# ACT copies a full bank, POOL adds twice: where the output additions of a fused retention and FP4 block are made

## The chip, the cores and the metric

One core of one Trainium2 chip. The metric is the device time of one execution in microseconds. The engines are called PE (TensorE), DVE (VectorE), ACT (ScalarE), POOL (GpSimd) and SP (SyncE, here only a DMA queue).

## The reference

Only what is computed matters here; the full reference also draws the inputs. The input is 8 x 1024 rows of 256 values.

```
x = L0_attn_X
xn = _layernorm(x, axis=-1)
x = x + _L0_attn_ref(xn, ...) + _L0_ffn_ref(xn, ...)
# _L0_attn_ref: retention with 8 heads of 32
Q = _xpos(einsum('bse,hed->bhsd', X, W_Q)); K = _xpos(..., downscale=True); V = ...
scores = einsum('bhsd,bhtd->bhst', Q, K) * D
Y = einsum('bhst,bhtv->bhsv', scores, V)
Yn = ((Y - mu) / sqrt(var + EPS)) * gn_weight + gn_bias
gate = X @ W_G; gate = gate * sigmoid(gate)
return gate * Yn @ W_O
# _L0_ffn_ref: every operand of a product is rounded to FP4 in blocks of 16
h = silu(fp4_linear(x, w_gate)) * fp4_linear(x, w_up)      # 704 wide
return fp4_linear(h, w_down)
```

## The kernel before

The kernel is written engine by engine: each engine has a program of its own, and semaphores tie them together. The order in which an engine works is the order of its code; nothing is scheduled by a planner.

The rows are cut into 64 tiles of 128 rows. Each engine runs `step(i)` for i from -4 to 63, and then `drain()`. A step is a software pipeline over several tiles: step i normalises and rounds tile i+1 or i+2, makes the large products of tile i, the retention and the quantisation of `h` for tile i-1, the down and output projections of tile i-2, and the final additions of tile i-3. Steps 0 to 2 also carry a part of the work on the weights, which the kernel rounds, transposes and splits itself. The weights of gate and up come in parts 0 to 2, those of down in parts 3 and 4. The last tile has no step behind it, so its later stages stand in `drain()`.

Every large product is made three times, with a high and a low part of each operand (`w_gu_hi`, `xqT_lo` and so on), so that fp32 accuracy comes out of the faster format. For the down and output projections the two weight parts lie side by side, `w_dn_both` and `w_out_both`. One product of 512 columns puts the high weights' result into the first half of a PSUM bank (`b_out`) and the low weights' into the second half (`b_out_lo`); both halves together are `b_out2`. The result of a tile is thus `b_out + b_out_lo + x`.

How those three are added is what the change is about. Before, ACT copies the second half into `y_low` (L820), DVE adds the first half and `x_in` into `y_half` (L619 in a step, L765 in the drain), and POOL adds the two into `y_out` (L448). SP then stores `y_out`. The semaphores are `out_ready` (PE has finished the bank), `halved` (ACT has copied), `summed` (the sum with `x_in` is there) and `added` (`y_out` is there). PE may begin the next tile's bank (L1119) when `summed` and `halved` are reached.

Names in the steps that follow: `h_quot` (POOL, L456) divides `h` by its block scale; ACT makes `h_magic` (L852); DVE makes `h_diff` (L691), `h_grid` (L705) and `hq` (L715) from it. `x_inv` (DVE, L695), `x_quot` (POOL, L479), `x_magic` (ACT, L868), `x_diff` (DVE, L711) do the same for the next tile's `x`. `qk` (POOL, L468) is the rotated query and key, which PE transposes at L1149. `y_part` (DVE, L748) and `z` (POOL, L512) end the group norm, `gate_gn` (POOL, L518) prepares it, `probs` (DVE, L759 and L630) masks the scores. `h_inv` (DVE, L632) inverts the block maxima of `h`. All of these stand in SBUF, except that `probs`, `y_half`, `y_part` and the first operand of a low part are read from PSUM.

In the set-up, `divide(n)` multiplies part n of the gate and up weights by its inverse scales, `round_off(n)` puts it onto the grid, and `centre_qkvg` takes the mean out of the projection weights, four column groups on ACT and four on POOL.

Of the kernel before, what the change touches and what calls it, by code (L numbers as in the profile page):

```python
# [16 lines left out]
P = 128  # L17
# [13 lines left out]
SLOTS = 8  # L31
# [37 lines left out]
def block_kernel(nc, x, xT, w_qkvg_d, w_o, gn_d, w_gu_d, w_down_d, cos_d, sin_d, causal_d, ident_d, by_head_d, out):  # L69
# [3 lines left out]
    with ExitStack() as ctx:  # L73
# [93 lines left out]
        y_half = sb("y_half", [P, 2, D])  # L167
        y_low = sb("y_low", [P, 2, D])
        y_out = sb("y_out", [P, 2, D])

# [267 lines left out]
        def _(pool):  # L438
# [4 lines left out]
            def residual(t):  # L443
# [4 lines left out]
                pool.tensor_tensor(y_out[:, t % 2, :], y_half[:, t % 2, :], y_low[:, t % 2, :], ALU.add).then_inc(added, 1)  # L448

            def step(i):  # L450
                if exists(i - 1):
# [22 lines left out]
                if exists(i - 3):  # L474
                    residual(i - 3)
                if exists(i + 1):
# [43 lines left out]
            def drain():  # L520
# [25 lines left out]
            def centre_qkvg():  # L546

                pool.wait_ge(qkvg_mean, 2)
                for j in range(4, 8):
                    pool.tensor_scalar(w_qkvg[:, j, :], w_qkvg[:, j, :], w_mean[:, j:j + 1], None,  # L550
                                       ALU.add).then_inc(qkvg_centred[1], 1)

# [23 lines left out]
        def _(dve):  # L576
# [36 lines left out]

            def first_half(t):
                dve.wait_ge(out_ready, t + 1)
                dve.wait_ge(halved, t + 1)
                if t >= 2:
                    dve.wait_ge(added, t - 1)
                dve.tensor_tensor(y_half[:, t % 2, :], b_out, x_in[:, t % SLOTS, :], ALU.add).then_inc(summed, 1)  # L619

            def step(i):
# [48 lines left out]
                if exists(i + 2):  # L670
                    t = i + 2
                    if t == 0:
                        dve.wait_ge(cleared, 2)
                    dve.wait_ge(x_stats, t + 1)
                    dve.bn_aggr(moments[:, 0:2], stats[:]).then_inc(x_moments, 1)  # L675
                    if i == -2:
                        largest(0)
                        invert(0)
                        divide(0)
                        largest(1)  # L680
                        round_off(0)
                        invert(1)
                        divide(1)
                if exists(i - 2):
# [76 lines left out]
            def residual(t):  # L761
                dve.wait_ge(out_ready, t + 1)
                dve.wait_ge(halved, t + 1)
                dve.wait_ge(added, t - 1)
                dve.tensor_tensor(y_half[:, t % 2, :], b_out, x_in[:, t % SLOTS, :], ALU.add).then_inc(summed, 1)  # L765
# [17 lines left out]
            def drain():  # L783
# [20 lines left out]
                z_low_part(t)  # L804
                residual(t)

# [7 lines left out]
        @block.scalar  # L814
        def _(act):
            def second_half(t):
                act.wait_ge(out_ready, t + 1)
# [4 lines left out]
            def step(i):  # L822
                if exists(i):
# [4 lines left out]
                    if exists(i - 3):  # L828
                        second_half(i - 3)
                    act.wait_ge(x_turned, t + 1)  # L830
                    act.activation(xqT_hi[:], tiles(b_xT[:, 0:D]), ACT.Copy).then_inc(xT_high, 1)
                    if i == 0:
                        low_part(2, 3)
                        high_part(4, 5)
                        qkvg_high_part(2)
                        magnitude(3)
                        qkvg_low_part(2)
                        out_high_parts()
# [16 lines left out]
                if exists(i + 1):  # L855
                    t = i + 1
                    if i == -1:
                        magnitude(0)
                        total_qkvg(0)
                        high_part(0, 1)  # L860
                        centre_qkvg()
                        magnitude(1)
                    if i == 0:
# [3 lines left out]
                    act.wait_ge(x_divided, t + 1)  # L867
                    act.activation(x_magic[:], x_quot[:], ACT.Abs, scale=GROW).then_inc(x_abs, 1)  # L868
                if exists(i):
                    t = i  # L870
# [58 lines left out]
            def drain():  # L929
# [16 lines left out]
                z_high_part(t)  # L946
                second_half(t)

# [35 lines left out]

            def centre_qkvg():

                act.wait_ge(qkvg_mean, 1)
                for j in range(4):
                    act.activation(w_qkvg[:, j, :], w_qkvg[:, j, :], ACT.Identity, bias=w_mean[:, j:j + 1],
                                   scale=1.0).then_inc(qkvg_centred[0], 1)  # L990

# [30 lines left out]
            for i in range(FIRST, 0):  # L1022
                step(i)
            high_part(2, 3)
            for i in range(TILES):
# [4 lines left out]
        def _(pe):  # L1030
# [5 lines left out]
            def step(i):  # L1036
# [16 lines left out]
                if exists(i):  # L1053
# [6 lines left out]
                    ins.then_inc(x_turned, 1)  # L1060
                    if i == 0:
                        turn_rest(2, 3)
                        turn(4, 5)
                        turn_qkvg(2)
                        turn_qkvg_rest(2)
# [42 lines left out]
                if exists(i - 2):  # L1108
# [117 lines left out]
            def turn_h(t):  # L1226
# [5 lines left out]
                ins.then_inc(h1_turned, 1)  # L1232

            def down_first(t):
                pe.wait_ge(hT_high0, t + 1)
                pe.wait_ge(summed, t)
                pe.wait_ge(halved, t)
                for k in range(3):
                    ins = pe.matmul(b_out2, hT_hi[:, k], w_dn_both[:, k], start=k == 0, stop=False)
                ins.then_inc(down_h0, 1)  # L1240

            def down_rest(t):
                pe.wait_ge(hT_high1, t + 1)
                for k in range(3, 5):
                    ins = pe.matmul(b_out2, hT_hi[:, k], w_dn_both[:, k], start=False, stop=False)
# [4 lines left out]
                pe.matmul(b_out2, hT_hi[:, 5], w_dn_both[:, 5], start=False, stop=False).then_inc(down_l1, 1)  # L1250
                pe.wait_ge(hT_low0, t + 1)
# [4 lines left out]
            def project_out(t):  # L1256
                pe.wait_ge(z_high, t + 1)
                for k in range(KD):
                    ins = pe.matmul(b_out2, zT_hi[:, k], w_out_both[:, k], start=False, stop=False)
                ins.then_inc(out_high, 1)  # L1260
# [174 lines left out]
```

## Time and profile before

| what | value |
|---|---|
| time, median of 3 executions | 883.75 us (883.57 to 884.05) |
| the profiled execution's own time | 883.53 us |
| its span | 881.7 us |
| PE busy | 856.0 us (97%) |
| DVE busy | 856.2 us (97%) |
| ACT busy | 462.3 us (52%) |
| POOL busy | 726.8 us (82%) |
| granted PE clock | full speed in all slices |
| HBM traffic | 37 GB/s over the span |

The span is the time from the first to the last event of the profiled execution; the time contains a little around it. Busy is the sum of an engine's operations, whoever waits for them. Two engines show 97% at once, so busy time alone does not say which of them sets the pace; the chain of work and the waits do.

### The profile page before, as it was taken

To read this page: it belongs to the slowest core of one execution; us is meant where nothing else is said; L and a number is where in the kernel's file an instruction comes from. 1 tells how busy PE (TensorE), PEld (TensorE's weight loads), DVE (VectorE), ACT (ScalarE), POOL (GpSimd) and SP (SyncE) were. 2 spreads that over 40 slices of the span, in tenths; PEclk is the share of its full clock that TensorE was granted. 3 is DMA by queue.
4 is the path that set the end of the run, shared out by engine and by line. 5 is a ranking of instruction groups with operands and counts; after the bars stand their busy time and mean duration, and the time that the engine had idled before them with its cause. 6 is when DMAs were issued, how large, how long until landed. Compare 5 with 4: busy or idle time off the path is not lost.

```text
span 881.7 us, 20677 instructions
## 1 busy us (share of the span) xinstructions
PE 856.0 (97%) x7858; PEld 708.7 (80%) x7858; DVE 856.2 (97%) x1883; ACT 462.3 (52%) x1210; POOL 726.8 (82%) x858
## 2 busy tenths in 40 slices
PE   3889999999999999999999999999999999999997
PEld 2668888888888888888888888888888888888885
DVE  7999999999999999999999999999999999999996
ACT  6655455555554555545545555555455554554553
POOL 5878888888888888888888888888888888888886
PEclk9999999999999999999999999999999999999999
DMA  9200110110111011011011011011001101100000
GB/s 339 82 2 19 38 38 19 38 36 21 36 37 29 28 37 33 23 38 37 19 38 37 20 37 37 23 34 37 29 28 36 34 23 38 37 19 26 13 7 25
DMA packets 30050, 33.63 MB, mean 38 GB/s; under 512 B 3328, under 2 KB 28672, under 8 KB 29696
## 3 DMA queue, kind: packets, MB, share of 16 engines
q1 hardware_dynamic: 29808, 32.26, 11.6%
q8 instruction: 62, 1.02, 0.5%
q14 instruction: 36, 0.29, 0.1%
q10 hardware_dynamic: 144, 0.07, 0.0%
HBM read 23.92 MB, written 8.39 MB: 37 GB/s over the span
## 4 chain that ended last, share of the span: by engine, by line
PE 93%; POOL 2%; DVE 2%; ACT 1%; issue 1%; DMA 0%; POOLq 0%; SPq 0%
PE quad L1034 12%; PE quad L1032 12%; PE quad L1033 12%; PE quad L1119 6%; PE bank L1032 5%; PE quad L1213 5%; PE quad L1095 4%; PE bank L1033 3%; PE quad L1203 3%; PE bank L1034 3%; PE quad L1189 3%; PE bank L1149 3%; PE quad L1198 3%; PE quad L1087 2%; PE quad L1075 2%; PE quad L1079 2%
## 5 line engine op out<-in xcount | busy, mean ns | idle before, releaser
L1032 PE MATMUL quad<-w_gu_hi,xqT_hi 128*128 128x512 f32 (+1 forms) x384 | 149.6, 390 | 0.0
L1034 PE MATMUL quad<-w_gu_hi,xqT_lo 128*128 128x512 f32 (+1 forms) x384 | 143.8, 374 | 0.0
L1033 PE MATMUL quad<-w_gu_lo,xqT_hi 128*128 128x512 f32 (+1 forms) x384 | 142.5, 371 | 0.0
L491 POOL TENSOR_TENSOR rstd<-var_eps,power 128x9 f32<-128x9 f32 x66 | 122.7, 1859 | 5.5
L456 POOL TENSOR_TENSOR h_quot<-h,h_inv 128x704 f32<-128x704 f32 x63 | 87.5, 1390 | 5.1
L468 POOL TENSOR_TENSOR qk<-qk_cos,qk_sin 128x512 f32<-128x512 f32 x64 | 83.6, 1307 | 5.9 <-PE bank L1105 0.7
L479 POOL TENSOR_TENSOR x_quot<-xn,x_inv 128x256 f32<-128x256 f32 x64 | 40.5, 633 | 57.8 <-DVE x_inv L695 57.5
L518 POOL TENSOR_TENSOR gate_gn<-gate,gn 128x512 f32<-128x512 f32 x63 | 81.7, 1298 | 0.0
L1034 PEld LDWEIGHTS quad<-w_gu_hi,xqT_lo 128*128 128x128 f32 x384 | 72.1, 188 | 11.4
L1033 PEld LDWEIGHTS quad<-w_gu_lo,xqT_hi 128*128 128x128 f32 x384 | 72.4, 189 | 10.8
L1032 PEld LDWEIGHTS quad<-w_gu_hi,xqT_hi 128*128 128x128 f32 x384 | 72.2, 188 | 11.0
L499 POOL TENSOR_TENSOR xT_lo<-xT_in,xT_hi 128x256 fp32r<-128x256 f32 x64 | 47.7, 745 | 40.4 <-ACT xT_hi L900 40.4
L912 ACT ACTIVATE xn<-x_in,x_shift,rstd 128x256 f32<-128x256 f32 x64 | 38.6, 602 | 77.6 <-POOL x_shift L503 77.6
L705 DVE SCALAR_TENSOR_TENSOR h_grid<-h_magic,h_diff 128x704 f16<-128x704 bf16 x63 | 75.5, 1199 | 0.0
L868 ACT ACTIVATE x_magic<-x_quot 128x256 bf16<-128x256 f32 x64 | 26.7, 417 | 82.8 <-POOL x_quot L479 82.8
L820 ACT ACTIVATE y_low<-quad 128x256 f32<-128x256 f32 x64 | 24.6, 385 | 82.1 <-PE quad L1051 78.5
L691 DVE SCALAR_TENSOR_TENSOR h_diff<-h_magic,h_quot 128x704 f32<-128x704 bf16 x63 | 67.3, 1069 | 0.0
L854 ACT ACTIVATE y_sq<-bank 128x256 f32<-128x256 f32 x63 | 24.2, 384 | 73.7 <-PE bank L1143 73.7
L489 POOL TENSOR_SCALAR var_eps<-moments 128x9 f32<-128x9 f32 x66 | 58.6, 888 | 3.6 <-DVE moments L675 3.2
L1119 PE MATMUL quad<-w_dn_both,hT_hi 128*128 128x512 f32 x186 | 59.7, 429 | 0.0
L1032 PE MATMUL bank<-w_qkvg_hi,xT_hi 128*128 128x512 f32 x128 | 57.1, 446 | 2.0 <-POOL xT_lo L499 1.9
L715 DVE TENSOR_TENSOR hq<-h_grid,h_scale 128x704 f32<-128x704 f16 x63 | 57.0, 904 | 0.0
(224 smaller groups left out, 2738.9 us busy)
## 6 DMA issues: line engine op xcount, KB each, us to landing
x_in<-in_x_dram SPq DMA_DIRECT2D x64, 128.0 KB, 2.2
xT_in<-in_xT_dram SPq DMA_DIRECT2D x64, 128.0 KB, 2.2
out_dram<-y_out SPq DMA_DIRECT2D x64, 128.0 KB, 1.7
sin<-const_sin_dram SPq DMA_DIRECT2D x1, 1792.0 KB, 11.0
raw<-in_w_gu_dram SPq DMA_DIRECT2D x2, 512.0 KB, 6.4
w_qkvg<-in_w_qkvg_dram SPq DMA_DIRECT2D x1, 1024.0 KB, 7.3
cos<-const_cos_dram SPq DMA_DIRECT2D x1, 896.0 KB, 7.1
raw<-in_w_down_dram SPq DMA_DIRECT2D x2, 352.0 KB, 7.8
```

The costliest lines, as they stand in the source:

```text
L456: pool.tensor_tensor(blocks(h_quot[:]), blocks(h[:]), spread(h_inv[:]), ALU.mult).then_inc(h_divided, 1)
L468: pool.tensor_tensor(qk[:], qk_cos[:], qk_sin[:], ALU.add).then_inc(rope_add, 1)
L489: pool.tensor_scalar(var_eps[:], moments[:, 1:], EPS, None, ALU.add).then_inc(var_ready, 1)
L491: pool.tensor_tensor(rstd[:, (t + 3) % RING, 0:1 + H], var_eps[:], power[:], ALU.pow).then_inc(rstd_ready, 1)
L518: pool.tensor_tensor(gate_gn[:, t % 2, :, :], gate[:].unsqueeze(1).broadcast_to([P, 2, D]), gn[:], ALU.mult).then_inc(gate_scaled, 1)
L691: dve.scalar_tensor_tensor(h_diff[:], h_magic[:], LEAST, h_quot[:], ALU.max, ALU.subtract).then_inc(h_diffed, 1)
L705: dve.scalar_tensor_tensor(h_grid[:], h_magic[:], LEAST, h_diff[:], ALU.max, ALU.subtract).then_inc(h_gridded, 1)
L715: dve.tensor_tensor(blocks(hq[:, 0:F]), blocks(h_grid[:]), spread(h_scale[:]), ALU.mult).then_inc(h_quant, 1)
L1032: pe.matmul(out, hi[:, k], w_hi[:, k], start=start, stop=False)
L1033: pe.matmul(out, hi[:, k], w_lo[:, k], start=False, stop=False)
L1034: return pe.matmul(out, lo[:, k], w_hi[:, k], start=False, stop=stop)
L1119: ins = pe.matmul(b_out2, hT_hi[:, k], w_dn_both[:, k], start=k == 0, stop=False)
```

## The change

In steps 3 to 63, ACT copies the whole bank into a new tile `y_both` (L814 of the changed kernel), and POOL makes both additions (L453 and L457). DVE's addition is gone from the step, and PE's wait for it too. The drain keeps the old split for tiles 61 and 62. For the last tile, PE puts the products with the high and the low weights on top of each other into `b_out` (`times_both`, two products of 256 columns for each of 512), and DVE adds `x_in` and writes `y_out` itself.

In the set-up, POOL instead of DVE divides part 1. ACT instead of POOL centres the second half of the projection weights. Three small reorderings on ACT and PE go with it.

The core of the diff (the pieces that only rename a call's place are left out):

```diff
+            def residual_of_both(t):
+                pool.wait_ge(halved, t + 1)
+                pool.tensor_tensor(y_half[:, t % 2, :], y_both[:, t % 2, 0:D], x_in[:, t % SLOTS, :], ALU.add).then_inc(summed, 1)
+                pool.wait_ge(summed, t + 1)
+                if t >= 2:
+                    pool.wait_ge(stored, 16 * (t - 1))
+                pool.tensor_tensor(y_out[:, t % 2, :], y_half[:, t % 2, :], y_both[:, t % 2, D:2 * D], ALU.add).then_inc(added, 1)
+
...
                 if exists(i - 3):
-                    residual(i - 3)
+                    residual_of_both(i - 3)
...
                     if i == -2:
                         size(0)
+                        divide(1)
                     if i == -1:
                         mean_qkvg(1)
-                        centre_qkvg()
...
                 residual(t - 1)
-                residual(t)
...
-                    if exists(i - 3):
-                        first_half(i - 3)
...
                         largest(1)
+                        invert(1)
                         round_off(0)
-                        invert(1)
-                        divide(1)
...
-                residual(t)
+                dve.wait_ge(out_ready, t + 1)
+                dve.wait_ge(added, t)
+                dve.wait_ge(stored, 16 * (t - 1))
+                dve.tensor_tensor(y_out[:, t % 2, :], b_out, x_in[:, t % SLOTS, :], ALU.add).then_inc(added, 1)
...
+            def both_halves(t):
+                act.wait_ge(out_ready, t + 1)
+                if t >= 2:
+                    act.wait_ge(added, t - 1)
+                act.activation(y_both[:, t % 2, :], b_out2, ACT.Copy).then_inc(halved, 1)
...
                     if exists(i - 3):
-                        second_half(i - 3)
+                        both_halves(i - 3)
...
                     if t >= 1:
-                        pe.wait_ge(summed, t)
                         pe.wait_ge(halved, t)
...
+            def times_both(t, part, both, start=False):
+                if exists(t + 1):
+                    return pe.matmul(b_out2, part, both, start=start, stop=False)
+
+                pe.matmul(b_out, part, both[:, 0, :], start=start, stop=False)
+                return pe.matmul(b_out, part, both[:, 1, :], start=False, stop=False)
```

What it does to the order on POOL inside a full step. Before, from `qk` on, between two tiles:

```order
L468 TENSOR_TENSOR qk<-qk_cos,qk_sin 128x512 [waits kv_ready,rope_cos]
L448 TENSOR_TENSOR y_out<-y_half,y_low 128x256 [waits stored,halved,summed]
L479 TENSOR_TENSOR x_quot<-xn,x_inv 128x256 [waits x_inverted]
L489 TENSOR_SCALAR var_eps<-moments 128x9 [waits x_moments,y_var]
L491 TENSOR_TENSOR rstd<-var_eps,power 128x9 [waits var_ready]
```

The same place after:

```order
L477 TENSOR_TENSOR qk<-qk_cos,qk_sin 128x512 [waits kv_ready,rope_cos]
L453 TENSOR_TENSOR y_half<-y_both,x_in 128x256 [waits halved]
L457 TENSOR_TENSOR y_out<-y_half,y_both 128x256 [waits stored,summed]
L488 TENSOR_TENSOR x_quot<-xn,x_inv 128x256 [waits x_inverted]
L498 TENSOR_SCALAR var_eps<-moments 128x9 [waits x_moments,y_var]
```

A second addition now stands between `qk` and `x_quot`, and it waits for the first.

On DVE, the stretch from the rotation's sine part to the low part of the rounded `x`, before:

```order
L632 TENSOR_SCALAR h_inv<-h_rec 128x44 [waits h_recip]
L638 SCALAR_TENSOR_TENSOR qk_sin<-bank,rstd,sin 128x512 [waits qk_ready]
L619 TENSOR_TENSOR y_half<-quad,x_in 128x256 [waits added,halved,out_ready]
L643 TENSOR_TENSOR xqT_lo<-bank,xqT_hi 128x256 [waits xT_high]
L646 SCALAR_TENSOR_TENSOR qk_cos<-bank,rstd,cos 128x512
```

And after:

```order
L626 TENSOR_SCALAR h_inv<-h_rec 128x44 [waits h_recip]
L632 SCALAR_TENSOR_TENSOR qk_sin<-bank,rstd,sin 128x512 [waits qk_ready]
L635 TENSOR_TENSOR xqT_lo<-bank,xqT_hi 128x256 [waits xT_high]
L638 SCALAR_TENSOR_TENSOR qk_cos<-bank,rstd,cos 128x512
L649 BN_STATS stats<-x_in 128x6 [waits loaded0]
```

The addition with `x_in` is gone, and the rest of DVE's step keeps its order.

On DVE in the set-up, where parts 0 and 1 of the gate and up weights (`raw`) are prepared, before:

```order
L580 TENSOR_REDUCE w_max<-raw 128x64 [waits w_landed1]
L598 SCALAR_TENSOR_TENSOR raw<-w_magic,raw 128x768 [waits w_abs]
L601 SCALAR_TENSOR_TENSOR w_magic<-w_magic,raw 128x768 [waits w_rounded0]
L605 TENSOR_TENSOR raw<-w_magic,w_scale 128x768 [waits w_sized,w_rounded0]
L586 RECIPROCAL w_rec<-w_max 128x64 [waits w_scaled1]
L588 TENSOR_SCALAR w_inv<-w_rec 128x64 [waits w_scaled1]
L593 TENSOR_TENSOR raw<-raw,w_inv 128x1024 [waits w_scaled1]
L625 TENSOR_REDUCE x_max<-xn 128x16 [waits x_normed]
```

After:

```order
L581 TENSOR_REDUCE w_max<-raw 128x64 [waits w_landed1]
L587 RECIPROCAL w_rec<-w_max 128x64 [waits w_scaled1]
L589 TENSOR_SCALAR w_inv<-w_rec 128x64 [waits w_scaled1]
L599 SCALAR_TENSOR_TENSOR raw<-w_magic,raw 128x768 [waits w_abs]
L602 SCALAR_TENSOR_TENSOR w_magic<-w_magic,raw 128x768 [waits w_rounded0]
L606 TENSOR_TENSOR raw<-w_magic,w_scale 128x768 [waits w_sized,w_rounded0]
L619 TENSOR_REDUCE x_max<-xn 128x16 [waits x_normed]
```

The inverse scales of part 1 are made before part 0 is rounded, and the division of 1024 columns has left DVE; on POOL it stands behind `size(0)`.

## Rows read from the trace of the kernel before

**Rows 1.** The page's chain that ended last, share of the span by engine.

```profile
PE 93%; POOL 2%; DVE 2%; ACT 1%; issue 1%; DMA 0%; POOLq 0%; SPq 0%
```

**Rows 2.** The chain in order of time: start us, us, what.

```profile
69.46 0.43 PE bank L1032
...
852.99 0.43 PE bank L1032
```

**Rows 3.** Timeline of one full step: start us, us, engine, operation [idle before <-releaser].

```profile
400.15 1.30 POOL L468 TENSOR_TENSOR qk<-qk_cos,qk_sin 128x512 f32<-128x512 f32 x1
...
401.42 0.73 POOL L448 TENSOR_TENSOR y_out<-y_half,y_low 128x256 f32<-128x256 f32 x1
...
401.81 1.09 DVE L691 SCALAR_TENSOR_TENSOR h_diff<-h_magic,h_quot 128x704 f32<-128x704 bf16 x1
...
402.82 0.16 DVE L695 TENSOR_SCALAR x_inv<-x_rec 128x16 f32<-128x16 f32 x1
...
403.06 0.62 POOL L479 TENSOR_TENSOR x_quot<-xn,x_inv 128x256 f32<-128x256 f32 x1 [0.91 <-DVE x_inv L695]
403.23 1.20 DVE L705 SCALAR_TENSOR_TENSOR h_grid<-h_magic,h_diff 128x704 f16<-128x704 bf16 x1
...
403.72 0.42 ACT L868 ACTIVATE x_magic<-x_quot 128x256 bf16<-128x256 f32 x1 [1.26 <-POOL x_quot L479]
...
404.36 0.41 DVE L711 SCALAR_TENSOR_TENSOR x_diff<-x_magic,x_quot 128x256 f32<-128x256 bf16 x1
...
405.27 0.60 ACT L879 ACTIVATE silu<-quad 128x512 f32<-128x512 f32 x1 [0.59 <-PE quad L1034]
...
408.17 0.41 DVE L748 TENSOR_TENSOR y_part<-bank,y_gain 128x256 f32<-128x256 f32 x1
...
408.92 0.73 POOL L512 TENSOR_TENSOR z<-y_part,gate_gn 128x256 f32<-128x256 f32 x1
...
409.07 0.69 DVE L759 TENSOR_TENSOR probs<-quad,causal 128x512 f32<-128x512 f32 x1 [0.16 <-PE quad L1213]
...
409.61 1.31 POOL L518 TENSOR_TENSOR gate_gn<-gate,gn 128x512 f32<-128x512 f32 x1
...
410.60 0.35 DVE L632 TENSOR_SCALAR h_inv<-h_rec 128x44 f32<-128x44 f32 x1
...
411.45 1.39 POOL L456 TENSOR_TENSOR h_quot<-h,h_inv 128x704 f32<-128x704 f32 x1
...
411.54 0.41 DVE L619 TENSOR_TENSOR y_half<-quad,x_in 128x256 f32<-128x256 f32 x1
...
413.28 1.30 POOL L468 TENSOR_TENSOR qk<-qk_cos,qk_sin 128x512 f32<-128x512 f32 x1
...
414.93 1.08 DVE L691 SCALAR_TENSOR_TENSOR h_diff<-h_magic,h_quot 128x704 f32<-128x704 bf16 x1
...
414.98 0.60 PE L1149 MATMUL bank<-ident,qk 128*128 128x128 f32 x4
```

**Rows 4.** Timeline, DVE in step 1 and both engines in the drain.

```profile
49.95 0.86 DVE L691 SCALAR_TENSOR_TENSOR h_diff<-h_magic,h_quot 128x704 f32<-128x704 bf16 x1
...
868.79 1.12 DVE L790 SCALAR_TENSOR_TENSOR h_diff<-h_magic,h_quot 128x704 f32<-128x704 bf16 x1 [0.67 <-ACT h_magic L934]
...
869.13 1.38 POOL L448 TENSOR_TENSOR y_out<-y_half,y_low 128x256 f32<-128x256 f32 x1
```

**Rows 5.** Timeline of the set-up.

```profile
12.14 1.24 DVE L593 TENSOR_TENSOR raw<-raw,w_inv 128x1024 f32<-128x1024 f32 x1
...
13.49 1.69 ACT L989 ACTIVATE w_qkvg<-w_qkvg,w_mean 128x256 f32<-128x256 f32 x4
...
23.11 5.47 POOL L550 TENSOR_SCALAR w_qkvg<-w_qkvg,w_mean 128x256 f32<-128x256 f32 x4
```

**Rows 6.** Timeline of the end.

```profile
877.47 0.40 PE L1263 MATMUL quad<-w_out_both,zT_lo 128*128 128x256 f32 x2
...
878.88 0.72 POOL L448 TENSOR_TENSOR y_out<-y_half,y_low 128x256 f32<-128x256 f32 x1 [3.23 <-DVE y_half L765]
```

More of the change, by code:

```diff
@@ L168, in block_kernel @@
         y_low = sb("y_low", [P, 2, D])
+        y_both = sb("y_both", [P, 2, 2 * D])
         y_out = sb("y_out", [P, 2, D])
@@ L544, in mean_qkvg @@
                 pool.tensor_scalar(w_mean[:, half], w_sum[:, half], -1.0 / D, None, ALU.mult).then_inc(qkvg_mean, 1)
[L546 to L551, printed above, removed]
             def size(n):
@@ L612, in low_difference @@
                     dve.tensor_tensor(lo, shaped(bank[HIGH_BANK[m]]), hi.bitcast(F32), ALU.subtract).then_inc(w_low[m], 1)
[L614 to L619, printed above, removed]
             def step(i):
@@ L763, in residual @@
                 dve.wait_ge(halved, t + 1)
-                dve.wait_ge(added, t - 1)
+                dve.wait_ge(added, TILES - 3 if t == TILES - 3 else t - 1)
                 dve.tensor_tensor(y_half[:, t % 2, :], b_out, x_in[:, t % SLOTS, :], ALU.add).then_inc(summed, 1)
@@ L833, in step @@
                         low_part(2, 3)
+                        qkvg_high_part(2)
                         high_part(4, 5)
-                        qkvg_high_part(2)
                         magnitude(3)
@@ L859, in step @@
                         total_qkvg(0)
+                        magnitude(1)
                         high_part(0, 1)
-                        centre_qkvg()
-                        magnitude(1)
                     if i == 0:
@@ L868, in step @@
                     act.activation(x_magic[:], x_quot[:], ACT.Abs, scale=GROW).then_inc(x_abs, 1)
+                    if i == -1:
+                        centre_qkvg(0)
                 if exists(i):
@@ L946, in drain @@
                 z_high_part(t)
-                second_half(t)
             def magnitude(n):
@@ L983, in total_qkvg, with centre_qkvg @@
                                    accum_out=w_sum[:, j:j + 1]).then_inc(qkvg_summed, 1)
-            def centre_qkvg():
-                act.wait_ge(qkvg_mean, 1)
-                for j in range(4):
+            def centre_qkvg(c):
+                act.wait_ge(qkvg_mean, c + 1)
+                for j in range(4 * c, 4 * c + 4):
                     act.activation(w_qkvg[:, j, :], w_qkvg[:, j, :], ACT.Identity, bias=w_mean[:, j:j + 1],
-                                   scale=1.0).then_inc(qkvg_centred[0], 1)
+                                   scale=1.0).then_inc(qkvg_centred[c], 1)
             def qkvg_high_part(*groups):
@@ L1023, in _ @@
                 step(i)
+            centre_qkvg(1)
             high_part(2, 3)
@@ L1061, in step @@
                     if i == 0:
+                        turn_qkvg(2)
                         turn_rest(2, 3)
                         turn(4, 5)
-                        turn_qkvg(2)
                         turn_qkvg_rest(2)
@@ L1238, in down_first @@
                 for k in range(3):
-                    ins = pe.matmul(b_out2, hT_hi[:, k], w_dn_both[:, k], start=k == 0, stop=False)
+                    ins = times_both(t, hT_hi[:, k], w_dn_both[:, k], start=k == 0)
                 ins.then_inc(down_h0, 1)
@@ L1244, in down_rest @@
                 for k in range(3, 5):
-                    ins = pe.matmul(b_out2, hT_hi[:, k], w_dn_both[:, k], start=False, stop=False)
+                    ins = times_both(t, hT_hi[:, k], w_dn_both[:, k])
                 ins.then_inc(down_h1, 1)
@@ L1249, in down_rest @@
                     pe.matmul(b_out, hT_lo[:, k], w_dn_hi[:, k], start=False, stop=False)
-                pe.matmul(b_out2, hT_hi[:, 5], w_dn_both[:, 5], start=False, stop=False).then_inc(down_l1, 1)
+                times_both(t, hT_hi[:, 5], w_dn_both[:, 5]).then_inc(down_l1, 1)
                 pe.wait_ge(hT_low0, t + 1)
@@ L1258, in project_out @@
                 for k in range(KD):
-                    ins = pe.matmul(b_out2, zT_hi[:, k], w_out_both[:, k], start=False, stop=False)
+                    ins = times_both(t, zT_hi[:, k], w_out_both[:, k])
                 ins.then_inc(out_high, 1)
```

## The prediction

> **What bounds the kernel now.** I read the chain of work first. Over the whole span 93% of it is TensorE (PE) [rows 1], and in order of time it is PE without a break from 69.46 us to 866 us; two of its steps begin at 69.46 and 852.99, sixty steps apart [rows 2], so a step takes 13.06 us on average, and one with all its products 13.12 (h_diff to h_diff, 401.81 to 414.93 [rows 3]). DVE is as busy as PE, but busy is not bound: the reader should look in [rows 3] for who waits. DVE's probs (L759) is released by PE; nothing of PE's waits for DVE or POOL. One margin matters: POOL's qk (L468) ends at 414.58, and PE's transposes of it start at 414.98, so POOL may come 0.3 us later per step before PE feels it. In the same rows POOL's x_quot (L479) waits 0.91 us for DVE's x_inv, and into that hole the second addition is put.
>
> **What also shows: POOL and DVE exclude each other.** h_diff (L691) takes 0.86 us where POOL is idle and 1.12 behind a POOL operation [rows 4]; in a step it is 1.09, and it ends 0.75 after POOL's y_out (402.15, 402.90); h_grid (L705, 1.20) ends 0.75 after x_quot (403.68, 404.43); and h_inv (L632, 0.35) ends 0.03 after gate_gn (410.92, 410.95) [rows 3]. The other way round, y_out issued at 869.13 behind an h_diff that ends at 869.91 takes 1.38 instead of 0.73: it ends 0.60 after it [rows 4]. So an operation of one holds back the other to almost its end. DVE operations with an operand in PSUM, as y_half and probs, show nothing of it.
>
> The Trainium skill, "SBUF — State Buffer", section "Who interferes with whom", says it so: "A DVE instruction with two SBUF inputs contends with a GpSimd instruction that reads SBUF", and the one that issues first blocks the other. By that rule, which the durations above agree with, both new additions compete with h_diff and h_grid; without it they would cost nothing, and the time would be that of the rival "it fits" below.
>
> **The full steps, part by part.** DVE loses y_half, 0.41 us a step. That is worth nothing by itself, since DVE waits for PE. ACT copies 512 columns instead of 256: a 512-wide copy takes about 0.60 (silu) against under 0.42 for 256 [rows 3]; the 0.2 us goes on to the ACT operations behind it until ACT next waits, as it does in every step (1.26 us before x_magic), so I cost it at nothing. PE no longer waits for DVE's half, and waits for ACT's as before: nothing. SP's loads wait for a later "summed", seven tiles ahead: nothing.
>
> POOL gets one more 0.73 us operation. The first addition takes y_out's place (401.42 to 402.15). The second is issued at about 402.22, but h_diff has been waiting since 401.81, gets in first and ends at 402.90, so the second addition ends at 402.90 + 0.60 = 403.50. x_inv (L695), due at 402.82, is held behind it to 403.53, x_quot starts 0.08 later, 403.61 and not 403.06, and h_grid is held behind x_quot as before. All of DVE that follows h_grid is 0.55 late in the first such step.
>
> Does that catch up? The dependencies close on themselves, and I add them up from y_part's start (408.17) to the next, all from [rows 3] but for the 0.60:
> - y_part to z: 0.41 + 0.08 (x_inv's end to x_quot's start) = 0.49. z no longer finds y_part ready, since y_part is later.
> - z to gate_gn 0.69, gate_gn to h_quot 1.84, h_quot to qk 1.83, qk to the first addition 1.27.
> - the addition 0.73, h_diff ends 0.75 later: 1.48
> - second addition 0.60, x_inv and the start of x_quot 0.03 + 0.08
> - x_quot 0.62, h_grid ends 0.75 later, x_diff starts 0.07 before that end (404.36), and from there to y_part (408.17) 3.81
>
> Sum 13.42 us. The same loop before has 0.08 + 0.08 in place of 0.71 behind h_diff: 12.87, which is 0.25 under PE's 13.12, and that is why PE set the pace. The change adds 0.55 and has 0.25 of room. Against 13.12 the loop is 0.30 longer, against the mean of 13.06 0.36 (PE's short steps do not shorten POOL's work); I take 0.34. It runs in steps 3 to 63, 61 of them: 61 x 0.34 = 20.7 us, less the 0.3 of margin in front of PE's transposes: **+20.4 us**. Bounds of a step's cost: 0 (if the second addition really fits) and 0.84 (next part), for the order at the lock is not certain.
>
> **Set-up.** POOL's four centring operations, 5.47 us, go to ACT (the like four took ACT 1.69) and DVE's division of 1024 columns, 1.24, goes to POOL [rows 5]; from POOL's 1.39 for 704 and 0.62 for 256 columns [rows 3] it is about 1.9 there, and DVE's rounding of part 0, issued just ahead of it, is held behind it and finishes some 2.4 us later than now. So the first turned weights come later, POOL's centring is off the path, and ACT, which now also carries those four in a row, becomes later for everything behind. Best case: 5.5 - 1.7 - 1.9 = 1.9 gained; worst: 2.4 lost. I take 0, in the middle, +-2.
>
> **The end.** The last tile's products go in pairs of 256 columns into one half (the same columns in all; nothing, at most 0.1). Then DVE alone adds x to it. Before, PE's last product ends at 877.87, and y_out at 879.60 after ACT, DVE and POOL in turn [rows 6]. Now: 877.87 + 0.08 + 0.41 = 878.36: **-1.2 us**. It is on the path, since the last store follows.
>
> **Sum.** The profiled execution took 883.5 us (span 881.7), the median is 883.75, so the base is the same within 0.2. 883.5 + 20.4 + 0 - 1.2 = **902.7 us**. Called no change is what lies within 0.2% (882.0 to 885.5).
>
> **Rivals.**
> 1. The lock goes the other way, 930 us or more. In the loop DVE reaches h_diff 6.76 - 0.16 (its wait for PE) - 0.41 (y_half gone) = 6.19 after y_part's start, POOL the first addition at 6.12: only 0.07 ahead. If h_diff goes first it ends at 7.05, the first addition at 7.65, x_inv at 7.68; the second addition, issued at 7.73, ends at 8.46, h_grid 0.75 later at 9.21, x_quot behind it at 9.21 + 0.49 = 9.70, and x_diff must wait for ACT's x_magic, 0.46 + 0.05 more: 10.21 + 3.81 = 14.02, perhaps 0.2 less by what then no longer collides. At 13.9, 0.84 a step: 883.5 + 51 - 1.2 = 933. For it: the margin is smaller than what I know of the moment at which the lock is taken. Against: POOL is ahead in both rows and sums.
> 2. It fits, 882.3 us (not slower): the second addition lies in x_quot's 0.91 us hole, ends at 402.95, and x_quot starts at 403.06 as before; only the end's 1.2 us show. It holds if the additions are not held by h_diff, or if the delay stays under the 0.25 of room. Against it are the four collisions above, y_out's 1.38 above all, which is the same operation on the same operands.
> 3. DVE was the bound after all: 61 x 0.33 less, 862 us. Against: PE's unbroken chain [rows 2] and DVE's wait at L759.
>
> **How the numbers follow.** Forecast 0.60 (its own range 893 to 912: 0.15 us a step in a loop of a dozen links, and 2 for set-up), rival 1 0.21, rival 2 0.16, rival 3 0.03. The range of 888 to 934 holds the first two, 0.81. Faster: rival 3, and 0.07 of rival 2, which lies near the bound: 0.10. Same: 0.09. Slower: 0.81.
>
> **What would show it.** In the profile after: the second addition at about 1.3 us, not 0.73; x_inv at 0.5 to 0.7, not 0.16; steps of 13.4 us; PE waiting for POOL's qk before its transposes, or for DVE's probs; in the chain, POOL and DVE with large shares from about the fifth tile on. If the additions take 0.73 each and the steps 13.1, I am wrong at the lock; if x_inv slips in ahead of the second addition and the order settles otherwise, the loop's length is wrong; if the first addition takes 1.3 too, it is rival 1. The last store should start about 0.5 us after PE's last product in any case.

## The result, and the profile after

The changed kernel takes **902.39 us** (median of 4 runs, 901.69 to 903.02). The kernel before, on the same chip, takes 883.90. The ratio is 1.021, 95% interval 1.0198 to 1.0222: slower by 18.5 us. Forecast were 902.7 us and a step of 13.42 us.

The profiled execution has a span of 899.9 us. The page's chain that ended last, by engine, answers to [rows 1]:

```profile
DVE 90%; PE 4%; ACT 2%; POOL 2%; issue 1%; DMA 1%; SPq 0%; POOLq 0%
```

TensorE no longer sets the end. The timeline of one step, POOL and DVE alone (start us, us, engine, operation, idle before and its releaser), answers to [rows 3]:

```profile
408.62 1.29 POOL L477 TENSOR_TENSOR qk<-qk_cos,qk_sin 128x512 f32<-128x512 f32 x1
409.87 0.73 POOL L453 TENSOR_TENSOR y_half<-y_both,x_in 128x256 f32<-128x256 f32 x1
409.96 1.39 DVE L682 SCALAR_TENSOR_TENSOR h_diff<-h_magic,h_quot 128x704 f32<-128x704 bf16 x1
410.68 1.28 POOL L457 TENSOR_TENSOR y_out<-y_half,y_both 128x256 f32<-128x256 f32 x1
411.27 0.71 DVE L686 TENSOR_SCALAR x_inv<-x_rec 128x16 f32<-128x16 f32 x1
412.06 0.62 POOL L488 TENSOR_TENSOR x_quot<-xn,x_inv 128x256 f32<-128x256 f32 x1
412.23 1.20 DVE L696 SCALAR_TENSOR_TENSOR h_grid<-h_magic,h_diff 128x704 f16<-128x704 bf16 x1
413.36 0.41 DVE L702 SCALAR_TENSOR_TENSOR x_diff<-x_magic,x_quot 128x256 f32<-128x256 bf16 x1
413.64 1.83 POOL L500 TENSOR_TENSOR rstd<-var_eps,power 128x9 f32<-128x9 f32 x1
413.69 0.90 DVE L706 TENSOR_TENSOR hq<-h_grid,h_scale 128x704 f32<-128x704 f16 x1
...
417.17 0.41 DVE L739 TENSOR_TENSOR y_part<-bank,y_gain 128x256 f32<-128x256 f32 x1
...
423.27 0.73 POOL L453 TENSOR_TENSOR y_half<-y_both,x_in 128x256 f32<-128x256 f32 x1
```

Read it from the top as a row of holds. The first addition (L453) starts 0.09 us before h_diff, which it holds: h_diff takes 1.39 us and ends 0.75 after it (410.60, 411.35). The second addition (L457) is issued while h_diff runs and ends 0.61 after it. x_inv, 16 columns and 0.16 us before, is held behind the addition and ends 0.02 after it. x_quot and h_grid follow as before. The next pair is different: rstd (POOL, only 9 columns) starts 0.05 ahead of hq, and neither holds the other. From first addition to first addition it is 13.40 us; the chain of additions from 75.40 to 851.48, 58 steps, gives 13.38 each.

What waits for it (waits in the window 400 to 800 us: total us, times, longest):

```profile
POOL z L521 <- DVE y_part L739: 7.8, 30, 0.3
PEld quad L1076 <- DVE probs L624: 7.4, 30, 0.3
PEld bank L1149 <- POOL qk L477: 1.7, 6, 0.4
```

TensorE now waits in every step for DVE's probs, for which nothing of it waited before. Of the set-up and the end, the timeline says (POOL's division, DVE's rounding and x_quot in step 2, then TensorE's last product and the last addition):

```profile
9.63 2.57 POOL L563 TENSOR_TENSOR raw<-raw,w_inv 128x1024 f32<-128x1024 f32 x1 [1.96 <-DVE w_inv L589]
...
10.44 2.57 DVE L602 SCALAR_TENSOR_TENSOR w_magic<-w_magic,raw 128x768 f16<-128x768 bf16 x1
...
63.74 0.62 POOL L488 TENSOR_TENSOR x_quot<-xn,x_inv 128x256 f32<-128x256 f32 x1 [1.07 <-DVE x_inv L686]
...
896.89 0.40 PE L1270 MATMUL quad<-w_out_both,zT_lo 128*128 128x256 f32 x2
...
897.33 0.42 DVE L799 TENSOR_TENSOR y_out<-quad,x_in 128x256 f32<-128x256 f32 x1 [1.18 <-PE quad L1270]
```

The same x_quot of step 2 starts at 63.30 in the kernel before. That the new set-up costs the difference of 0.44 us does not follow: in the runs below this x_quot starts at 63.48 to 63.69 with the old set-up and at 63.19 to 64.35 with the new one (those with x_inv behind h_diff, as here). At the end y_out is done 0.46 us after TensorE's last product, where it was 1.73 [rows 6].

### The profile page after: what moved, and what is told of

Its sections match the earlier page's. It is cut to its first block, busy times and chain, and to the rows that moved or that the text cites. A ratio compares the mean times of both kernels' runs of the same rounds, so it can differ in the third digit from the quotient of the medians.

```text
span 899.9 us, 20626 instructions
## 1 busy us (share of the span) xinstructions
PE 873.5 (97%) x7866; PEld 707.9 (79%) x7866; DVE 881.8 (98%) x1821; ACT 470.8 (52%) x1213; POOL 807.3 (90%) x915
## 4 chain that ended last, share of the span: by engine, by line
DVE 90%; PE 4%; ACT 2%; POOL 2%; issue 1%; DMA 1%; SPq 0%; POOLq 0%
DVE h_diff L682 9%; DVE h_grid L696 7%; DVE hq L706 6%; DVE h_max L735 5%; DVE qk_cos L638 4%; DVE qk_sin L632 4%; DVE x_inv L686 4%; DVE h L720 4%; DVE probs L624 4%; DVE xq L726 4%; DVE probs L750 4%; DVE hT_lo L677 3%; DVE zT_lo L655 3%; DVE xqT_lo L635 2%; DVE x_diff L702 2%; DVE stats L649 2%
## 5 line engine op out<-in xcount | busy, mean ns | idle before, releaser
L682 DVE SCALAR_TENSOR_TENSOR h_diff<-h_magic,h_quot 128x704 f32<-128x704 bf16 x63 | 86.5, 1373 | 0.0
L457 POOL TENSOR_TENSOR y_out<-y_half,y_both 128x256 f32<-128x256 f32 x61 | 76.9, 1261 | 4.8
L814 ACT ACTIVATE y_both<-quad 128x512 f32<-128x512 f32 x61 | 36.4, 597 | 62.6 <-PE quad L1052 62.6
L521 POOL TENSOR_TENSOR z<-y_part,gate_gn 128x256 f32<-128x256 f32 x63 | 46.6, 740 | 16.4 <-DVE y_part L739 16.4
L508 POOL TENSOR_TENSOR xT_lo<-xT_in,xT_hi 128x256 fp32r<-128x256 f32 x64 | 57.8, 903 | 2.6 <-ACT xT_hi L901 2.6
```

What stands on the lines that cost most here:

```text
L682: dve.scalar_tensor_tensor(h_diff[:], h_magic[:], LEAST, h_quot[:], ALU.max, ALU.subtract).then_inc(h_diffed, 1)
```

## The experiments

Two theories. **L**, the prediction's: POOL and DVE exclude each other, so what a POOL operation costs depends on what DVE runs beside it and on who is in first. Held means, here and below, that an operation's record has begun but its work has to wait for the other engine's operation to end. **W**: the changed kernel is slower because POOL has 0.73 us more to do in a step, wherever it does it. In the diffs below, + is the experiment, ... stands for what is left out, and `first_sum` and `second_sum` are `residual_of_both` cut in two. Where a step's length is given, it is the distance of two like POOL operations near 410 us.

| kernel | step, us | median, us | ratio to before, 95% |
|---|---|---|---|
| before | 13.10 | 883.57 to 883.90 | |
| changed | 13.38 | 902.39 | 1.0198 to 1.0222 |
| full steps alone | 13.38 | 903.92 | 1.0212 to 1.0240 |
| set-up and end alone | 13.11 | 883.14 | 0.9980 to 0.9998 |
| end alone | 13.11 | 882.43 | 0.9979 to 0.9997 |
| DVE's addition left out | 13.11 | 883.61 | 0.9988 to 1.0010 |
| second addition 128 wide | 13.11 | 885.48 | 1.0011 to 1.0030 |
| write in place of the second addition | 13.10 | 882.86 | 0.9981 to 1.0000 |
| first addition 0.2 us later | 13.79 | 924.68 | 1.0451 to 1.0482 |
| x_quot between the additions | 13.69 | 920.62 | 1.0403 to 1.0431 |
| x_inv ahead of h_diff | 13.55 | 911.62 | 1.0299 to 1.0327 |
| second addition behind y_gain | 13.24 | 893.47 | 1.0097 to 1.0127 |
| the same, old set-up | 13.23 | 892.91 | 1.0089 to 1.0123 |
| the same, x_inv ahead of h_diff | 13.11 | 882.57 | 0.9980 to 0.9998 |

### Which part of the change costs

**Full steps alone**: the kernel before with both_halves, residual_of_both and without first_half.

> The kernel before with the full steps of the change alone; set-up and end as before. Theory L (the lock between POOL and DVE, the forecast): steps of 13.39 us as in the changed kernel, 902.4 + 1.2 (the end's gain is gone) - 0.4 (the set-up's loss is gone) = 903.2 us. Rival S (set-up or end carry part of the loss): clearly below 902.

Measured 903.92 (902.81 to 904.36).

**Set-up and end alone**: the changed kernel with the full steps of before.

> The changed kernel with the full steps of before: only set-up and end are changed. Theory L: steps back at 13.06 us on average, 883.8 - 1.2 + 0.4 = 883.0 us. Rival S: well above 884.

Measured 883.14 (882.01 to 883.68).

**End alone**: the kernel before with the last tile in pairs and DVE's single addition.

> The kernel before with the change of the last tile alone (products in pairs, DVE writes y_out). Both theories: one ACT copy and one POOL addition leave the last chain, 883.8 - 1.2 = 882.6 us. If the pairs of products cost PE time, it is nearer to 883.8.

Measured 882.43; the spans are 880.6, and 881.3 with the new set-up too, against 881.7 before. So the full steps carry the whole loss, and the end gains 1.1. The set-up gives 0.7 of that back by these spans, and 1.0 in the pair with the second addition behind y_gain further below (890.9 and 891.9; by the medians 0.7 and 0.6). On top of the new full steps, set-up and end together gain 1.1 (901.0 to 899.9), which leaves nothing for it. It costs between 0 and 1.0.

**DVE's addition left out**, which takes from DVE what the change takes, and gives POOL nothing more (the first half of the bank is not added; the waits for DVE's sum and DVE's additions in the drain are gone too):

```diff
-                pool.tensor_tensor(y_out[:, t % 2, :], y_half[:, t % 2, :], y_low[:, t % 2, :], ALU.add).then_inc(added, 1)
+                pool.tensor_tensor(y_out[:, t % 2, :], x_in[:, t % SLOTS, :], y_low[:, t % 2, :], ALU.add).then_inc(added, 1)
...
-                    if exists(i - 3):
-                        first_half(i - 3)
```

> The kernel before without DVE's addition y_half in any tile: POOL adds y_low and x_in instead (the first half of the bank is left out of the output). Theory L: DVE's freed 0.33 to 0.41 us a step are worth nothing, since PE sets the pace: 883.8, less about 0.5 at the end, 883.3 us. Rival D (DVE is the bound): 61 x 0.33 less, 862 us.

Measured 883.61, no change. The trace (DVE's groups, window 400 to 800 us: busy us, mean ns, idle before) shows where the 0.33 us went:

```profile
L688 DVE SCALAR_TENSOR_TENSOR h_diff<-h_magic,h_quot 128x704 f32<-128x704 bf16 x31 | 42.7, 1378 | 0.0
```

In the kernel before this group has a mean of 1079 ns: DVE comes to h_diff earlier and stands there, held by POOL's addition, 0.30 longer.

### What in the second addition costs

**Second addition 128 columns wide** (the rest of the second half is not added; the first addition writes y_out itself):

```diff
-                pool.tensor_tensor(y_out[:, t % 2, :], y_half[:, t % 2, :], y_both[:, t % 2, D:2 * D], ALU.add).then_inc(added, 1)
+                pool.tensor_tensor(y_out[:, t % 2, :], y_both[:, t % 2, 0:D], x_in[:, t % SLOTS, :], ALU.add).then_inc(summed, 1)
+                pool.wait_ge(summed, t + 1)
+                pool.tensor_tensor(y_out[:, t % 2, 0:P], y_out[:, t % 2, 0:P], y_both[:, t % 2, D:D + P], ALU.add).then_inc(added, 1)
```

> The changed kernel with the second addition only 128 columns wide (the low half's other 128 columns are left out). From 1.30 us for 512 and 0.73 for 256 columns it is about 0.45 us long, 0.28 less. Theory L with the loop of 13.42: 13.14, just at PE's pace, 884 to 887 us. Rival W: POOL's work per step falls by 0.28 as well, the same. It tests the size of the room, not the cause.

```profile
416.22 1.39 DVE L682 SCALAR_TENSOR_TENSOR h_diff<-h_magic,h_quot 128x704 f32<-128x704 bf16 x1
416.94 0.99 POOL L457 TENSOR_TENSOR y_out<-y_out,y_both 128x128 f32<-128x128 f32 x1
417.53 0.43 DVE L686 TENSOR_SCALAR x_inv<-x_rec 128x16 f32<-128x16 f32 x1
418.04 0.62 POOL L488 TENSOR_TENSOR x_quot<-xn,x_inv 128x256 f32<-128x256 f32 x1
```

Measured 885.48. The narrower addition is held by h_diff all the same and ends 0.32 after it instead of 0.61. That 0.29 is about the prediction's excess of the loop over TensorE's pace, and the step is back at 13.11. It is not quite TensorE's pace again: the chain of this run is 75% DVE and 20% TensorE. In the kernel before, every eighth step (h_diff to h_diff) is down to 12.85; here no full step before the last tiles is under 13.01, and 885.48 is 2.3 above the set-up and end alone. So 13.11 is the loop's own length now, where 13.42 less 0.28 gave 13.14. As its expectation says, this run sizes the room; W gives the same time.

**A write in place of the second addition** (the second half is not added, the first addition writes y_out as above; the 512 columns written are of a buffer no longer used):

```diff
+                pool.memset(raw[:, 0:512], 0.0).then_inc(added, 1)
```

> The changed kernel with a memset of 512 columns in place of the second addition (the low half is left out of the output): POOL writes SBUF and reads none. Theory L, if only reads exclude each other: the memset is not held by h_diff, and x_inv is not held by it unless writes count too; steps at 13.1 us, 883 us. Rival W: as long as the memset is about as long as the addition, 13.3 to 13.4 us a step, 898 to 902 us. If it is held like the addition (about 0.5 us longer than its own length), reading is not what counts.

```profile
414.37 0.74 POOL L455 TENSOR_TENSOR y_out<-y_both,x_in 128x256 f32<-128x256 f32 x1
414.70 1.15 DVE L682 SCALAR_TENSOR_TENSOR h_diff<-h_magic,h_quot 128x704 f32<-128x704 bf16 x1
415.16 0.53 POOL L457 MEMSET raw<- 128x512 f32 x1
```

Measured 882.86. The write begins and ends inside h_diff: neither holds the other (h_diff still ends 0.74 after the addition). The Trainium skill, "SBUF — State Buffer", section "Who interferes with whom", says that DVE's two-input instructions contend with a POOL instruction that reads, "not with one that only writes it". This trace agrees. So POOL's sequence may have one more instruction in this place at no cost; but this run takes away duration as well (0.53 against 0.73), and alone it does not refute W. The next two do.

### Who is in first

**First addition 0.2 us later**, behind a write of 128 columns that holds nobody:

```diff
             def residual_of_both(t):
+                pool.memset(raw[:, 0:P], 0.0)
                 pool.wait_ge(halved, t + 1)
```

> The changed kernel with a memset of 128 columns ahead of the first addition, to make it some 0.1 to 0.2 us later; in the changed kernel it begins only 0.09 us before h_diff. Theory L: h_diff now goes first, the first addition is held too (1.3 us), and the order of rival 1 of the prediction comes up: 13.8 to 14.0 us a step, 928 to 941 us. Rival W: 0.1 to 0.2 us a step more, 908 to 915 us.

```profile
419.09 0.20 POOL L452 MEMSET raw<- 128x128 f32 x1
419.20 0.88 DVE L683 SCALAR_TENSOR_TENSOR h_diff<-h_magic,h_quot 128x704 f32<-128x704 bf16 x1
419.26 1.42 POOL L454 TENSOR_TENSOR y_half<-y_both,x_in 128x256 f32<-128x256 f32 x1
420.00 0.71 DVE L687 TENSOR_SCALAR x_inv<-x_rec 128x16 f32<-128x16 f32 x1
420.76 0.74 POOL L458 TENSOR_TENSOR y_out<-y_half,y_both 128x256 f32<-128x256 f32 x1
420.96 1.29 DVE L697 SCALAR_TENSOR_TENSOR h_grid<-h_magic,h_diff 128x704 f16<-128x704 bf16 x1
421.46 1.27 POOL L489 TENSOR_TENSOR x_quot<-xn,x_inv 128x256 f32<-128x256 f32 x1
...
423.21 0.42 DVE L703 SCALAR_TENSOR_TENSOR x_diff<-x_magic,x_quot 128x256 f32<-128x256 bf16 x1 [0.96 <-ACT x_magic L868]
```

A write of 0.2 us costs 22.3 us. h_diff starts 0.06 us before the first addition and is free of it (0.88), the first addition takes 1.42, and x_quot is now the one that h_grid holds (1.27), so that DVE waits 0.96 for x_magic. This is rival 1 of the prediction, link by link. The step of 13.79 lies just under the 13.8 to 14.0 given, and the time under the 928 to 941 given and under rival 1's 930: from x_diff to y_part (426.81) it is 3.60 here, not the 3.81 that was taken over, and xq in that stretch takes 0.42 where it took 0.60. Rival 1 had named such a saving ("perhaps 0.2 less"). W, with 908 to 915, is refuted.

**x_inv ahead of h_diff** in the changed kernel, so that an input of x_quot is ready earlier and nothing else changes:

```diff
+                if exists(i + 1):
+                    t = i + 1
+                    dve.wait_ge(x_recip, t + 1)
+                    dve.tensor_scalar(x_inv[:], x_rec[:], SIX, 1e12, ALU.mult, ALU.min).then_inc(x_inverted, 1)
                 if exists(i - 1):
                     t = i - 1
                     dve.wait_ge(h_abs, t + 1)
...
-                    dve.wait_ge(x_recip, t + 1)
-                    dve.tensor_scalar(x_inv[:], x_rec[:], SIX, 1e12, ALU.mult, ALU.min).then_inc(x_inverted, 1)
```

> The changed kernel with DVE's x_inv moved ahead of h_diff, nothing else: something that comes earlier. Theory L: second addition ends 1.35 after the first's end as before; x_inv is done, so x_quot is issued right behind it, but h_grid has been waiting longer and gets in first. It ends 0.75 after the second addition, x_quot 0.49 later, x_magic and x_diff then 0.5 after that: x_diff starts 0.36 later in the loop than in the changed kernel, 13.75 a step, some 922, slower than the changed kernel although only one operation comes earlier; range 910 to 930. Rival D (only dependencies count: x_quot's wait for x_inv was on the path and is gone): 13.1 a step, 883, or at least under 902.

```profile
414.18 0.72 POOL L453 TENSOR_TENSOR y_half<-y_both,x_in 128x256 f32<-128x256 f32 x1
414.27 0.67 DVE L682 TENSOR_SCALAR x_inv<-x_rec 128x16 f32<-128x16 f32 x1
414.86 0.88 DVE L686 SCALAR_TENSOR_TENSOR h_diff<-h_magic,h_quot 128x704 f32<-128x704 bf16 x1
414.98 1.35 POOL L457 TENSOR_TENSOR y_out<-y_half,y_both 128x256 f32<-128x256 f32 x1
...
415.99 1.10 DVE L698 SCALAR_TENSOR_TENSOR h_grid<-h_magic,h_diff 128x704 f16<-128x704 bf16 x1
416.30 1.27 POOL L488 TENSOR_TENSOR x_quot<-xn,x_inv 128x256 f32<-128x256 f32 x1
...
418.05 0.43 DVE L704 SCALAR_TENSOR_TENSOR x_diff<-x_magic,x_quot 128x256 f32<-128x256 bf16 x1 [0.97 <-ACT x_magic L869]
```

Measured 911.62, 9 us slower than the changed kernel because one operation comes earlier: the sign was forecast, and no account by dependencies alone, or by the amount of work, gives it. x_quot is issued right behind the second addition, but h_grid was issued 0.3 earlier and gets in first. From the first addition's start (414.18) to x_diff it is 3.87, against 3.49 in the changed kernel (409.87 to 413.36), as forecast (0.36 more). The expected 922 was 10 too high, because the rest of the step was taken over at 3.81; it is 3.61 here (x_diff at 418.05, y_part at 421.66), since by the later x_diff POOL and DVE miss each other there: xq takes 0.41, in the changed kernel 0.60.

### Moving the second addition

**x_quot between the additions**:

```diff
                     pool.tensor_tensor(blocks(x_quot[:]), blocks(xn[:, t % 2, :]), spread(x_inv[:]), ALU.mult).then_inc(x_divided, 1)
...
+                if exists(i - 3):
+                    second_sum(i - 3)
```

> The changed kernel with x_quot between POOL's two additions; the same work on every engine. Theory L: x_quot goes at once after x_inv, as before; the second addition is held behind h_grid, where var_eps was held anyway, and the steps are back at about 13.1 us: 883.0 us, 882 to 886. Rival W (POOL has simply too much work in a step, wherever it stands): unchanged, 902 us.

```profile
419.82 0.63 POOL L490 TENSOR_TENSOR x_quot<-xn,x_inv 128x256 f32<-128x256 f32 x1 [0.91 <-DVE x_inv L690]
419.99 1.21 DVE L700 SCALAR_TENSOR_TENSOR h_grid<-h_magic,h_diff 128x704 f16<-128x704 bf16 x1
420.40 1.39 POOL L459 TENSOR_TENSOR y_out<-y_half,y_both 128x256 f32<-128x256 f32 x1
421.12 0.96 DVE L706 SCALAR_TENSOR_TENSOR x_diff<-x_magic,x_quot 128x256 f32<-128x256 bf16 x1
...
422.00 0.88 DVE L710 TENSOR_TENSOR hq<-h_grid,h_scale 128x704 f32<-128x704 f16 x1
422.29 2.28 POOL L504 TENSOR_TENSOR rstd<-var_eps,power 128x9 f32<-128x9 f32 x1
```

Measured 920.62 where L was said to give 883.0: the expectation missed by 37 us, and in the wrong direction. x_inv comes free (0.16), but the expectation overlooked the next two-input operation of DVE. The second addition is now held by h_grid (1.39, ending 0.59 after it), in its turn holds x_diff (0.96 instead of 0.41), and rstd, late, finds hq in front of it (2.28 instead of 1.83). The chain is 77% POOL, 13.69 us a step. W is wrong here too: it has the same work on every engine as the changed kernel, and is 18 us slower.

**Second addition behind y_gain**, where DVE runs h_max, a reduction of one input, and POOL used to wait 0.69 us for xT_hi:

```diff
                     pool.tensor_tensor(heads(y_gain[:]), heads(gate_gn[:, t % 2, 0, :]), spread(rstd[:, (t + 3) % RING, 1:1 + H], HD), ALU.mult).then_inc(gain_ready, 1)
+                if exists(i - 3):
+                    second_sum(i - 3)
                 if exists(i + 1):
                     t = i + 1
                     pool.wait_ge(x_high, t + 1)
```

> The changed kernel, with POOL's second addition moved behind y_gain, ahead of xT_lo: where POOL idled 0.69 us in the kernel before and where DVE runs h_max, which reads one operand. The additions, their number and widths stay. Theory L (a POOL operation next to a two-input or small float32 operation of DVE costs, its mere length doesn't): the second addition takes 0.73 to 0.8, xT_lo comes 0.1 to 0.2 later, y_part is not held; h_diff stays at up to 1.4, x_inv returns to 0.16, and steps to 13.1 us: 883.5 + 0.4 for set-up - 1.2 = 882.7, range 881.5 to 884.5. Rival W (0.73 us more POOL work is what costs): 902. Rival M (any splitting of the two additions lengthens the loop as in the kernel with x_quot between them): 910 to 920.

> The kernel before with the full steps of the kernel above (second addition behind y_gain) and the new end, without the new set-up: L 882.3, the same as the end alone, since PE sets the pace again and the time freed on DVE is worth nothing; range 881.2 to 884. W 901.

```profile
412.40 0.60 DVE L730 TENSOR_TENSOR xq<-x_grid,x_scale 128x256 f32<-128x256 f16 x1
412.68 0.92 POOL L459 TENSOR_TENSOR y_out<-y_half,y_both 128x256 f32<-128x256 f32 x1
412.93 0.87 DVE L739 TENSOR_REDUCE h_max<-h 128x44 f32<-128x704 f32 x1
...
420.30 1.39 DVE L686 SCALAR_TENSOR_TENSOR h_diff<-h_magic,h_quot 128x704 f32<-128x704 bf16 x1
...
421.86 0.62 POOL L490 TENSOR_TENSOR x_quot<-xn,x_inv 128x256 f32<-128x256 f32 x1 [0.92 <-DVE x_inv L690]
```

Measured 893.47, and 892.91 with the old set-up: half of the loss is gone, though the amount of work is the same, but not all, as L was said to give. The second addition itself behaves nearly as expected (0.92, of which 0.19 is hold by xq, whose end it follows by 0.60; h_max is not held). What was overlooked is POOL's own sequence. Its wait of 0.69 for xT_hi is filled now, and its one remaining wait, 0.92 for x_inv, is not slack: x_inv comes behind h_diff, and h_diff is held by POOL's own first addition. POOL's sequence of 12.3 (11.7 busy, the rest in the gaps between operations) and a wait of 0.92 that POOL causes itself make the 13.24 us of a step, and the chain is 78% POOL. Rival M (910 to 920) is refuted as W (902) is: split additions need not cost what they cost around x_quot. What POOL has to do in a step does count here, but only through the place of its wait.

**The same with x_inv ahead of h_diff** was made to test that reading.

> The kernel with the second addition behind y_gain and the new end alone (892.9), with DVE's x_inv moved ahead of h_diff. In that kernel the chain in order of time is POOL's own sequence, 13.24 us a step, with 0.92 us of it the wait for x_inv, which comes behind h_diff, which comes behind the first addition. Theory L (the loop is dependencies plus the lock): x_quot no longer waits for x_inv but is held by h_diff, which has been waiting longer and gets in first; it ends 0.49 after h_diff's end, 0.3 earlier than there. POOL's loop falls to 12.94, under PE's 13.12, steps are 13.1: 882.4, range 881.3 to 885. Rival W (POOL's amount of work sets it, and the wait was only slack): 892.9 as there. Rival F (h_diff now slips in ahead of the first addition, x_inv being in its way): the loop gets shorter still, the same 882.4 by the end; if instead x_quot slips in ahead of h_diff, h_diff comes 0.5 later and steps are 13.4 or more, 900 or above.

```profile
414.45 0.73 POOL L453 TENSOR_TENSOR y_half<-y_both,x_in 128x256 f32<-128x256 f32 x1
...
415.12 0.88 DVE L705 SCALAR_TENSOR_TENSOR h_diff<-h_magic,h_quot 128x704 f32<-128x704 bf16 x1
415.29 1.20 POOL L490 TENSOR_TENSOR x_quot<-xn,x_inv 128x256 f32<-128x256 f32 x1
```

Measured 882.57, the chain is 94% TensorE, the step 13.11. x_quot is held by h_diff (ends 0.49 after it) instead of waiting for x_inv behind it, and ends 2.04 after the first addition's start where it was 2.27. h_diff did not slip in ahead of the first addition: x_inv stood there instead (0.43, till 415.21), and h_diff, starting behind both, is free at 0.88. The same edit of DVE's order that costs 9 us in the changed kernel gains 10.3 here; what differs is which pair of operations stands side by side afterwards.

Three kernels that compute the whole result are faster than before, each by 0.1% and by an interval below 1: this one (882.57), the end alone (882.43), and set-up and end alone (883.14). This one can't be told from the end alone, whose gain (1.1 by the spans, 1.2 by the medians) it contains: while TensorE sets the pace, moving both additions to POOL in the full steps was at best free.

## Why the prediction was right

- **The step.** Forecast 13.42 us, measured 13.38. The links measured: h_diff ends 0.75 after the first addition (0.75), the second addition 0.61 after h_diff (0.60), x_inv 0.02 after that (0.03), x_diff to y_part 3.81 (3.81). The experiments show this term: without the full steps the loss is gone, and a second addition that ends 0.29 earlier brings the step back to 13.11.
- **The mean step** was taken as 0.34 over the kernel before; 13.38 - 13.06 = 0.32, and 61 x 0.32 = 19.5, less the 0.3 in front of the transposes 19.2, against 20.4. The full steps alone cost 19.3 by the spans (881.7 to 901.0) and 20.3 by the medians. The 0.3 itself stands in no row: from qk's end to the transposes it is 0.40 there.
- **Set-up.** Taken 0 +- 2, measured between 0 and 1.0. The division on POOL was put at 1.9 and takes 2.57: the rounding operation ahead of it on DVE (L599) held it, which the sum left out, and it held the next one (L602, 2.57). The rounding of the part ends 2.6 later than before (forecast 2.4); 1.0 of that is a later start, behind the inverse scales of part 1. What the new ACT and POOL work cancels of that was not taken apart.
- **The end.** Forecast -1.2, measured -1.1 by the spans of the end alone.
- **Sum.** 883.5 + 19.2 - 1.1 = 901.6, and 0 to 1.0 more for the set-up; the profiled execution took 901.7. The median, 902.39, lies 0.3 under the forecast. That close it is luck, since the terms are known to 1 us only; the mechanism and the step, 0.04 off, are not.
- **The margin of 0.07** between the first addition and h_diff is 0.09 in the trace. It held in 60 of the 61 steps; in a late one, at 864.85, the first addition takes 1.39 and the second 0.74. Rival 1, then, was near: a write of 0.2 us makes it true in all steps but the first, at 924.7 us, not 933. The sum behind the margin came out (6.19 forecast for DVE, 6.18 measured) although y_half's place on DVE is 0.33, as rival 3 has it, and not 0.41.
- **Rival 2** is wrong in this place. Behind y_gain, and with x_inv moved ahead of h_diff as well, the time is 882.57, as it gave; behind y_gain alone it is 893.47.
- **Rule of the lock.** That an operation of one holds back the other to almost its end, and that whoever issues first blocks, is not so for every pair. rstd reads 9 columns and takes 1.83. It starts 0.04 to 0.05 ahead of hq, which reads two operands from SBUF, and hq takes 0.90; where it starts 0.5 ahead (first addition 0.2 us later) hq takes 0.88. The other way round hq does hold rstd (2.28 instead of 1.83). The loop of the prediction does not rest on this pair.
- **Rival 3** fell with DVE's addition left out: 883.61.
- **What would show it**: the second addition at 1.28, x_inv at 0.71 and the waits of TensorE are there. Wrong was that the chain would show POOL and DVE with large shares. It shows DVE at 90% and POOL at 2%. TensorE's wait was for probs, in every step, and for qk in 6 of 30. The time in which POOL holds DVE is inside the durations of h_diff, x_inv and h_grid, and a chain counts it as DVE's work.

**Left open**: what decides when both engines issue still closer together. In the rows shown, whoever started first, by 0.05 us (rstd and hq) or more, or had been waiting longer, was in first; no closer pair is shown. Open too is how long an operation of POOL really holds: for rstd it is not the length of its record.

## What to carry to other kernels

Before moving an operation between POOL and DVE, write down for each place what the other engine runs there, whether it is held when POOL is in first, and how many inputs it reads from SBUF (here also x_inv, with one input, was held); a hole in one engine's timeline is no room if the other one, when released, starts an operation that excludes it. A wait is slack only if what ends it doesn't depend on the waiting engine's own earlier work: POOL's 0.91 us for x_inv looked free and was of its own making. Where two engines arrive at the lock within 0.1 us of each other, price both orders, since a later edit of 0.2 us ahead can flip them, here for 22 us.

## What the runs showed of the hardware

- A held operation ends less than its own duration after the one that held it: h_diff 0.75 where it takes 0.88 unhindered, an addition 0.59 to 0.61 where it takes 0.73, x_quot 0.48 to 0.49 where it takes 0.62. It is as if the hold ended some 0.13 us before the holder's record does.
- Not every POOL operation that reads SBUF holds DVE for its length: beside rstd (9 columns, 1.83 us, in first by 0.05 or 0.5) hq takes 0.90 or 0.88. Behind hq, rstd itself takes 2.28.
- A float32 operation of 16 columns and one input (x_inv, 0.16) is held as a large one is (0.71). A reduction of one input (h_max, 0.87) runs beside POOL's addition unhindered.
- A write by POOL neither holds nor is held: 128 columns 0.20, 512 columns 0.53.
